# Perceiver block on one core: squares summed in two rounded parts, inputs loaded in pieces, and a reordered end of the cross-attention

## The reference, cut to what matters

```python
x = x + _L0_xattn_ref(_layernorm(x), ctx_1024, Wq, Wk, Wv, Wo, gq, gk)   # 16 heads of 128
x = x + _L0_attn_ref(_layernorm(x), W_qkv, W_out, b_out)
x = x + _L0_ffn_ref(_layernorm(x), W_gate, W_qkv)

# inside _L0_xattn_ref
q = (hidden_states @ Wq).reshape(B, Sq, H, D)
k = (encoder_hidden_states @ Wk).reshape(B, Skv, H, D)
v = (encoder_hidden_states @ Wv).reshape(B, Skv, H, D)
q = q * rsqrt(mean(q * q) + eps) * gq          # rmsnorm over D, and so k with gk
attn = softmax(einsum('bqhd,bkhd->bhqk', q, k) / sqrt(D))
out = einsum('bhqk,bkhd->bqhd', attn, v).reshape(B, Sq, H * D) @ Wo
```

## Time and profile before

| what | us |
|---|---|
| median of 3 runs | 1482.8 (1478.25 to 1483.11) |
| the profiled execution, its own time | 1480.01 |
| its span in the profile | 1478.0 |
| query loop, first product to last output | 22.7 to 139.2 |
| cross-attention's first instruction on PE | 142.7 |

### The profile page before, as it was taken

One profiled execution on the slowest core, in us unless ns is written; L12 is line 12 of the kernel. 1 busy time (PEld: TensorE's weight loads), 2 busy tenths in 40 slices (PEclk: granted clock), 3 DMA queues, 4 the chain that ended last, 5 costly groups with the idle time before them and its releaser, 6 DMA issues. The chain is left out here.

```text
span 1478.0 us, 31543 instructions
## 1 busy us (share of the span) xinstructions
PE 1386.3 (94%) x5980; PEld 936.6 (63%) x5980; DVE 1259.4 (85%) x5006; ACT 1202.5 (81%) x4843; POOL 982.6 (66%) x1505
## 2 busy tenths in 40 slices
PE   5997999999999999999999999999999999966886
PEld 4664666666666666666666666666666666854554
DVE  6776888998989898889989898998998998756985
ACT  5886889898898989898988988898989887535763
POOL 4000788888989898889889898988888885010000
PEclk9998999999999999999999999999999999986998
DMA  4000000000000000000000000000000001000000
GB/s 143 38 1 1 1 2 24 4 21 16 10 23 1 24 1 23 2 23 2 23 13 13 23 1 25 1 23 2 23 1 27 22 30 64 1 1 1 8 7 16
DMA packets 9849, 25.30 MB, mean 17 GB/s; under 512 B 736, under 2 KB 6016, under 8 KB 9520
## 3 DMA queue, kind: packets, MB, share of 16 engines
q1 hardware_dynamic: 9648, 23.49, 4.4%
HBM read 22.44 MB, written 1.05 MB: 16 GB/s over the span
## 5 line engine op out<-in xcount | busy, mean ns | idle before, releaser
L1014 ACT ACTIVATE c_unused<-c_prod 124x128 f32<-124x128 f32 x1664 | 493.1, 298 | 83.6 <-DVE c_prod L1238 77.5
L1554 POOL TENSOR_TENSOR c_acc<-c_acc,c_prob 123x1024 f32<-123x1024 f32 (+1 forms) x192 | 461.9, 2406 | 23.9 <-ACT c_prob L1021 23.2
L1249 DVE CUSTOM_DVE_ANT_0 c_multiplied<-psK,c_c 124x128 f32<-124x128 f32 x1664 | 381.5, 285 | 57.0 <-PE psK L809 57.0
L808 PE MATMUL psK<-wkh,c_cTh 128*124 128x512 f32 x832 | 413.5, 497 | 10.9 <-DVE c_cTl L1277 9.2
L828 PE MATMUL psO<-c_prob,raw 123*128 123x512 f32 (+1 forms) x832 | 392.1, 594 | 0.0
L1238 DVE TENSOR_TENSOR c_prod<-psK,c_c 124x512 f32<-124x512 f32 x416 | 286.0, 688 | 53.4 <-PE psK L809 40.1
L809 PE MATMUL psK<-wkl,c_cTh 128*124 128x512 f32 x832 | 329.6, 396 | 0.0
L1014 ACT ACTIVATION_READ_ACCUMULATOR c_unused<-c_prod 124x1 f32 x1664 | 311.3, 187 | 0.0
L1260 DVE TENSOR_TENSOR c_prob<-psS,c_ss 124x512 f32<-124x512 f32 x416 | 265.7, 680 | 0.5 <-POOL c_ss L1537 0.5
L1021 ACT ACTIVATE c_prob<-c_prob,shift 124x1024 f32<-124x1024 f32 x208 | 236.6, 1137 | 0.4 <-DVE c_prob L1260 0.4
L808 PEld LDWEIGHTS psK<-wkh,c_cTh 128*124 128x124 f32 x832 | 154.2, 185 | 114.7 <-DVE c_ss L1249 47.5
(11 more groups left out here) (314 smaller groups left out, 2165.2 us busy)
## 6 DMA issues: line engine op xcount, KB each, us to landing
raw<-in_ctx SPq DMA_DIRECT2D x16, 799.5 KB
raw<-in_L_xattn_Wq SPq DMA_DIRECT2D x3, 512.0 KB, 9.5
xs<-in_x SPq DMA_DIRECT2D x1, 1024.0 KB, 5.8
big<-in_L_xattn_Wk SPq DMA_DIRECT2D x1, 1024.0 KB, 8.7
c_prod<-in_L_xattn_Wo SPq DMA_DIRECT2D x1, 1024.0 KB, 5.3
out<-s_y SPq DMA_DIRECT2D x8, 128.0 KB, 1.7
big<-in_L_ffn_W_qkv SPq DMA_DIRECT2D x1, 768.0 KB, 12.5
raw<-in_L_xattn_Wv SPq DMA_DIRECT2D x1, 768.0 KB, 4.1
```

What stands on the lines that cost most here:

```text
L808: nc.tensor.matmul(psK[0:ROWS, c % 2, :], cTh[:, slot, :], T.wkh[:, cols], start=True, stop=False)
L1014: last = nc.scalar.activation(unused[:, j, :], prod[:, k % 2, c // 2, j * CD:(j + 1) * CD], ACT.Copy, accum_out=ss[:, k % 2, 0, h:h + 1])
L1249: last = nc.vector.tensor_tensor_reduce(multiplied[:, j, :], psK[0:ROWS, 1, cols], c2[:, k % NT, :], 1.0, 0.0, ALU.mult, ALU.add, ss[:, k ...
L1554: nc.gpsimd.tensor_tensor(acc[0:rows, batch % 2, :], acc[0:rows, batch % 2, :], prob[0:rows, probs(s), :], ALU.add).then_inc(S.acc, 1)
```

## The change

In `queries`:

- `x` comes in four transfers, each quarter of `Wq` in two, and the gains are loaded from ACT's queue. The statistics and the centring run in two halves of four pairs, so that ACT's guess of the inverse root for one half lies beside DVE's work on the other.
- Turning `Wk` and its high and low parts move from the prelude into the loop (items 0 and 1), into four banks of their own. The high parts of the second to fourth quarter of `Wq` move to items 0, 1 and 3, their low parts to POOL beside items 0 to 11, in pieces of 256 columns.
- The sum of squares is no longer one float32 product: POOL makes a rounded copy `squareh` of `square` (an addition of a zero column) and the remainder `squarel`, and PE adds two fp32r products with `onesr`. It is done at stage o and no longer at stage m; the logarithm follows it at the head of ACT's step.
- DVE writes the Newton factor over `psS` (PSUM) and not into the SBUF tile `scaled`; `root` reads it there. DVE's order in a step is `qgl(n)`, factor, `root`, output. `psS` comes free after `root`, not after the factor.
- `raw` is zeroed in four parts at items 20 to 23. The gain reduction moves from items 28 and 30 to 25 and 28.

In `end`: `matrices(1)` and `segment(0)` come before `denominators` of the last batch on PE, and the logarithms, exponentials and Newton steps after the parts of segment 1 on ACT and DVE. `turn(2)` waits for the end of the Newton step.

```diff
@@ sync
-            sp.dma_start(T.xs[:, :, :], dram["x"].rearrange("b q c -> (b q) c").rearrange("(n p) c -> p n c", p=P)).then_inc(S.x, 16)
+            x = dram["x"].rearrange("b q c -> (b q) c").rearrange("(n p) c -> p n c", p=P)
+            for j, sem in enumerate(x_there):
+                sp.dma_start(T.xs[:, PW * j:PW * (j + 1), :], x[:, PW * j:PW * (j + 1), :]).then_inc(sem, 16)
@@ gpsimd
+            def step(n, m, o):
+                if m is None:
+                    return
+                pool.wait_ge(S.square, m + 1)
+                if m >= 2:
+                    pool.wait_ge(S.total, m - 1)
+                nc.gpsimd.tensor_tensor(squareh[:, m % 2, :], square[:, m % 2, :], blank[:, :].broadcast_to([P, BANK]), ALU.add).then_inc(S.squareh, 1)
+                pool.wait_ge(S.squareh, m + 1)
+                nc.gpsimd.tensor_tensor(squarel[:, m % 2, :], square[:, m % 2, :], squareh[:, m % 2, :].bitcast(F32), ALU.subtract).then_inc(S.squarel, 1)
+                if low_part(m) is not None:
+                    q, k, part = low_part(m)
+                    pool.wait_ge(S.wqh, WC + q)
+                    nc.gpsimd.tensor_tensor(halved(wql[:, :, quad(q)])[:, k, part, :], wq(q)[:, k, part, :],
+                                            halved(wqh[:, :, quad(q)])[:, k, part, :].bitcast(F32), ALU.subtract).then_inc(S.wql, 1)
+                if m in ZERO_AT:
+                    nc.gpsimd.memset(T.raw[:, ZERO[ZERO_AT.index(m)]], 0.0).then_inc(S.zeroed, 1)
@@ tensor
-                if m is not None:
-                    pe.wait_ge(S.square, m + 1)
-                    if m >= 2:
-                        pe.wait_ge(S.newton, m - 1)
-                    nc.tensor.matmul(psS[:, m % 2, :], T.ones[:, :], square[:, m % 2, :], start=True, stop=True).then_inc(S.total, 1)
+                    if n < len(WK_AT):
+                        for q in WK_AT[n]:
+                            transpose_wk(q)
                 if o is not None:
+                    pe.wait_ge(S.squarel, o + 1)
+                    if o >= 2:
+                        pe.wait_ge(S.root, o - 1)
+                    nc.tensor.matmul(psS[:, o % 2, :], onesr[:, :], squareh[:, o % 2, :], start=True, stop=False)
+                    nc.tensor.matmul(psS[:, o % 2, :], onesr[:, :], squarel[:, o % 2, :], start=False, stop=True).then_inc(S.total, 1)
@@ vector
-                    nc.vector.scalar_tensor_tensor(scaled[:, :], psS[:, o % 2, :], float(D * EPS), half[:, :], ALU.add, ALU.mult).then_inc(S.newton, 1)
+                    nc.vector.scalar_tensor_tensor(psS[:, o % 2, :], psS[:, o % 2, :], float(D * EPS), half[:, :], ALU.add, ALU.mult).then_inc(S.newton, 1)
@@ tensor, end
             def end(i, batch):
-                denominators(i, batch, 0)
-                pe.wait_ge(W.vTl, 2)
-                denominators(i, batch, 1)
                 matrices(1)
                 segment(0)
+                denominators(i, batch, 0)
+                denominators(i, batch, 1)
+                segment(1)
                 turn(2)
                 turn(3)
-                segment(1)
                 segment(2)
@@ vector, end (scalar alike)
             def end(i, batch):
+                for n in range(HB):
+                    weighed_low(n)
                 product_low(1)
                 next_segment(0)
+                for half in range(2):
+                    newton_start(i, batch, half)
+                    newton_end(i, batch, half)
                 wo_low(2)
+                next_segment(1)
                 v_low(2)
```

More of the change, by code:

```diff
@@ L181, in load_context @@
     sp.dma_start(raw[FULL:ROWS, b, 0:REST, :], one[:, FULL * NT:SKV, :]).then_inc(sems[1], 16)
-PREP_SEMS = ("x gains wk wq0 wq1 wq2 wq3 consts gprod made stats moments centred lnT lnTh lnTl wkT wkTh wkTl wqh wql "
-             "gram gramh graml zeroed context m8 m2 sel causal iota selb wgate wqkv turn turned gT gtop gall")
+PREP_SEMS = ("x0 x1 x2 x3 gains wk wq0 wq1 wq2 wq3 consts gprod made stats moments centred lnT lnTh lnTl wkT wkTh wkTl wqh wql "
+             "wql0 onesr blank gram gramh graml zeroed context m8 m2 sel causal iota selb wgate wqkv turn turned gT gtop gall")
 Q_SLOTS = 3
 X_SLOTS = 2 * BANK // DIM
-ITEM_SEMS = "q square qgh qgl total log y half newton root qw out"
+ITEM_SEMS = "q square squareh squarel qgh qgl total log y half newton root qw out"
 def queries(nc, T, psum, dram):
@@ L337, in _ @@
                     last.then_inc(S.lnT, 1)
[L338 to L341, removed]
             def gram(q):
+                pe.wait_ge(S.wkTl, KC)
                 if q >= 2:
@@ L389, in step @@
                     for k in range(WC):
+                        if n == 0:
+                            pe.wait_ge(S.wql0, k + 1)
                         for w, x in ((wqh, xTh), (wql, xTh), (wqh, xTl)):
@@ L451, in _ @@
             act.wait_ge(S.consts, 5)
-            act.wait_ge(S.made, 1)
+            act.wait_ge(S.made, 2)
+            nc.scalar.activation(onesr[:, :], T.ones[:, :], ACT.Copy).then_inc(S.onesr, 1)
             def step(n, m, o):
+                if o is not None:
+                    act.wait_ge(S.total, o + 1)
+                    nc.scalar.activation(log[:, :], psS[:, o % 2, :], ACT.Ln, scale=1.0 / D, bias=T.eps[:, :]).then_inc(S.log, 1)
                 if n is not None:
@@ L494, in _ @@
                 nc.vector.tensor_copy(T.maskb[rows, :], maskc[rows, b, :])
[L495 to L512, removed]
-                                        wkTh[:, HB * q:HB * (q + 1), :].bitcast(F32), ALU.subtract).then_inc(S.wkTl, 1)
@@ L515, in _, with statistics @@
-            for q in range(2):
-                wk_low(q)
-            for j in range(NPAIR // PW):
+            dve.wait_ge(S.consts, 2)
+            nc.vector.tensor_copy(T.identb[:, :], T.ident[:, :]).then_inc(S.made, 1)
+            def statistics(half):
+                for i in range(half * NPAIR // 2, (half + 1) * NPAIR // 2):
+                    if i % PW == 0:
+                        dve.wait_ge(x_there[i // PW], 16)
+                    nc.vector.bn_stats(stats[:, i, :], T.xs[:, i, :]).then_inc(S.stats, 1)
@@ L528, in _ @@
             nc.vector.tensor_scalar(T.gcol[:, 1:2], T.gcol[:, 0:1], float(SCALE), None, ALU.mult).then_inc(S.made, 1)
-            dve.wait_ge(S.made, 1)
-            nc.vector.tensor_copy(T.identb[:, :], T.ident[:, :]).then_inc(S.made, 1)
+            for j in range(NPAIR // PW):
+                turned_low(j)
             def gram_low(q):
```

174 lines of the change are left out of this document (108 added, 66 removed).

## The result

The changed kernel takes 1465.5 us (median of 4 runs, 1464.35 to 1465.67), the kernel before beside it 1482.9 (median of 4, 1478.25 to 1483.11): a ratio of 0.9888, 95% interval 0.9869 to 0.9908.

A forecast was written before the change was run, and what follows sets the result against it. PE was taken to bound the query loop; 8.2 (loop) + 0.4 (start) + 0.3 (tail) + 0.1 (end of the cross-attention) = 9.0 us gained, from 1482.8 to 1473.8, say 1474, range 1466 to 1481.

The forecast's parts named there:

- the likeliest case: Whole kernel: 9 us gained, mostly in the query loop, own range 1470 to 1478; chance 0.55.
- PE gives up the bound: Query loop: PE's item falls to 2.57 us, so POOL (3.1), then DVE (2.8) bound it.
- The first rival: Query loop: PE stays the bound at 2.65 an item, 14 gained, 1469 us; chance 0.18.
- With the same 4% the later items are 2.9: Query loop from item 12: waits and handoffs keep their 4% share, giving 2.9 us an item.
- the 2.8 that it starts from: Query loop from item 12: DVE's chain of pitches, 0.66 + 3 x 0.71 = 2.79, taken as 2.8 us.
- 3.1 for items 2 to 11 (POOL ...): Early query loop: POOL's pair plus `Wq`'s low part bounds each item at 3.1 us, range 3.0 to 3.4.
- the cheaper sum: Query loop: two rounded products cost 0.47 us in place of 0.93; loop forecast 91.2 against 99.4, 8.2 gained.
- The factor in PSUM at no extra, and no `root` held up by POOL: DVE in the query loop: writing PSUM costs nothing extra and avoids up to 1.28 us of exclusion with POOL.
- Start: 0.4 gained of 3.7: Before the loop: first product 3.7 us earlier, at 19.0, but item 2's square only 0.4 earlier, at 30.4.
- Tail 0.3, end of the cross-attention 0.1: Behind the last square 0.3 us gained; at the cross-attention's end 0.1, between -1.5 and 3.
- waits 0.2 to 1.6: End of the cross-attention: `segment(2)` waits 0.2 to 1.6 us for its first input, giving gain back.
- the slower rival: Query loop: PE's granted clock falls; all ten first items would give +12, 1495 us; this or another loss 0.07.

The follow-up runs named there:

- the last experiment: The changed kernel with DVE's share of segment 1 put ahead of the low part of `Wo`'s third quarter: 1464.9 us, ratio 0.9897.

## Why the prediction was right or wrong

Faster, by 17.4 us of medians where 9 were forecast; 1465.5 is half a us under the range's low end of 1466. The mechanism of the likeliest case held in the main, and two of its terms, the loop's gain and the start's, were too small.

- *PE gives up the bound.* Right for the ordinary items, where ACT's 2.66 and DVE's 2.72 are above PE's 2.57; in the items with a gram PE still sets the pace. The first rival had PE at 2.65, and its time, 1469, came closer than mine because 2.65 happens to lie near 2.66 and 2.72: in the mechanism it was wrong. Neither engine overlaps better than its pitches, as that rival asked: both keep them, without pauses.
- *"With the same 4% the later items are 2.9".* This is the step that failed, together with the 2.8 that it starts from. DVE's work is 2.72, since the fourth of its pitches, from an output to the next `qgl`, is 0.61 and not another 0.71. And the 4% of waits were the waste of the old order, and went with it: the float32 sum in the new order has items of 2.96, PE's own work, where the kernel before mostly has 3.15. The nineteen later items took 55.9, forecast 55.1 + 4.4 = 59.5. At 2.72 they are 51.7, which leaves 4.2 for the additional parts, beside the forecast 4.4.
- *"3.1 for items 2 to 11 (POOL ...)".* Right in the sum, 31.85 against 31.7, by luck in part. POOL's work there is 3.07 an item (1.04, 1.29, 0.74), 30.7 of the 31.85, but 0.2 more on each changed nothing. The intervals are 2.66 to 2.88 for the ordinary items, 3.60 with `Wq`'s high part and 3.14 with one more copy on ACT, and 4.16 twice with a gram on PE.
- *Where the gain of the loop is from.* I gave it all to the cheaper sum. It is 6.0; the other 5.7 came with the order, the factor's place and, 0.5 of it, the weights', which I had priced at nothing in the loop.
- *The factor in PSUM at no extra, and no `root` held up by POOL.* Right: 0.69 and 0.69, and 4.4 us worse the other way.
- *Start: 0.4 gained of 3.7.* Too small. The first product came at 18.45, forecast 19.0; the square of item 2 at 28.26, forecast 30.4. Between them lie 9.8 us and not 11.4: the turnings of `Wk` cost less than I took, since from 23.3 on PE runs at full speed, and half of them lie behind that:

```profile
18.45 0.79 PE L433 MATMUL psK<-q_xTh,q_wqh 128*128 128x512 f32 x1 [0.55 <-DVE q_xTl L583]
...
19.04 0.63 PE L433 MATMUL psK<-q_xTh,q_wql 128*128 128x512 f32 x1
19.46 0.63 PE L433 MATMUL psK<-q_xTl,q_wqh 128*128 128x512 f32 x1
...
23.59 0.39 PE L433 MATMUL psK<-q_xTl,q_wqh 128*128 128x512 f32 x1
23.82 0.40 PE L433 MATMUL psK<-q_xTh,q_wqh 128*128 128x512 f32 x1
```

  Products are 0.43 apart until then and 0.23 after; in the kernel before the mean clock up to 30.8 was 0.63, and the clock stayed at 0.50 until 28.7, 6.0 us behind its first product in place of 4.9.
- *Tail 0.3, end of the cross-attention 0.1.* 0.06 and 1.15 (59.33 to 58.18 from the last weighing on; the main loop ahead of it, which the change doesn't touch, is 1092.66 and 1092.64 in these two profiles). The forecast of the place was right: `segment(2)` "waits 0.2 to 1.6", 1.27 measured. That the low clock lasted 3.4 us and not 6.8, which is worth up to 1.7, was outside the sum.
- *The clock in the loop.* It stayed at 1.00, so the slower rival has no ground here.

## What to carry to other kernels

When a dominant instruction gets cheaper, don't carry the old waits over as a share: recompute each engine's own work, take the longest without pauses as the floor, and ask whether the new order still has a reason to pause. A little added work on one engine at a time, read in the profile of the stretch, tells in which items an engine binds; engines that are within a few per cent of one another take turns. Where a buffer's release moves to a later instruction (the factor into `psS`), check which engine's head waits for that release: here the factor in PSUM is worth 4.4 us in one order, and in the other it goes with a loop 18.6 us longer than that of the kernel before.

## What the runs showed of the hardware

**A window's clock of 1.00 can mean that nothing was recorded.** The trace keeps a list of stretches with their granted clock. In the changed kernel it begins at 23.4 us, in the kernel before at 18.5, in the others between 21.5 and 24.8, and ahead of its first entry a window shows 1.00 (first row of the table of windows, 18.45 to 28.26). But until 23.3 products of 512 columns start 0.43 apart, just as in the kernel before, where 0.50 is recorded, and from there on 0.23. In each of the eight traces where products run across the first entry the spacing changes within 0.3 us of it. So at the start of a kernel the distance of the starts is to be read.

**The last block has two times.** Behind the next layer's first product the instructions are the same in all kernels. They took 183.3 to 183.7 us in nine of the fourteen profiles, 185.6 in one, and 187.1 to 188.4 in four. The changed kernel's last stretches, then those of the kernel with the old end:

```profile
1439.20:1449.20 10.00, 7.17 (x65) 5.02 (x65) 5.41 (x21) 4.04 (x13) 0.00 (x0) 1.00 0.04 14
1449.20:1459.20 10.00, 5.77 (x60) 4.92 (x60) 3.58 (x8) 2.25 (x3) 0.00 (x0) 0.55 0.04 15
```

```profile
1440.20:1450.20 10.00, 8.11 (x27) 5.53 (x28) 3.64 (x18) 3.46 (x8) 0.00 (x0) 0.66 0.04 14
1450.20:1460.20 10.00, 4.42 (x62) 3.23 (x61) 5.76 (x11) 2.75 (x7) 0.00 (x0) 0.81 0.05 15
1460.20:1467.00 6.80, 3.25 (x40) 3.00 (x38) 1.33 (x4) 1.03 (x2) 0.00 (x0) 0.50 0.06 19
```

The clock falls once in the nine profiles and twice in the five others. The slower way costs 3.4 to 4.0 us in three of them, 1.9 in one, and 4.7 or more in one where the low stretch ahead of it, too, is longer (37.5 us, in the others 34.1). The four runs of the last experiment lie in two pairs, 1463.1 and 1463.2, 1466.5 and 1467.1; whether it is the same cause was not shown, since only one of them is profiled. An edit anywhere ahead shifts the block in time and may change which of the two is met.

**The main loop varies too.** From the cross-attention's first product to the last weighing no kernel was edited, yet it takes 1092.5 to 1093.4 us in six profiles and 1093.5 to 1097.5 in eight. These eight have, some 17 us into it, a second stretch of 3.4 us at clock 0.50, which the six lack. It can cost at most 1.7, so it doesn't account for the whole of the three longest (1094.6, 1095.0 and 1097.5); what else they meet isn't known. So differences under 5 us between these kernels are read in the stretch that was edited.
